# A fused state-space and expert layer: new instruction orders in its first six and last three groups, and more identity products on TensorE at the start

## The reference, cut to what matters

```python
mod = (_silu(L0_c) @ L0_wmod).reshape(8, 6, 1, -1)
sa, ca, ga, sb, cb, gb = ...                     # ga, gb: kept at least 0.25 from zero
h = _layernorm(x) * (1 + ca) + sa
# state part
v, gate = split(h @ W_in + b_in)
hs[t] = sigmoid(A) * hs[t-1] + v[t]              # a scan over the 1024 rows of a batch
x = x + ga * ((sigmoid(gate) * hs * C) @ W_out + b_out)
# expert part
h = _layernorm(x) * (1 + cb) + sb
p = softmax(h @ gate_w + gate_b); p = p * (p >= 0.1); p = p / sum(p)
x = x + gb * sum_e p[:, e] * (h @ expert_w[e] + expert_b[e])     # 8 experts
```

## Time and profile before

| what | value |
|---|---|
| median of 3 runs | 209.23 us (208.98 to 212.89) |
| the profiled execution, its own time | 209.71 us |
| its span, first to last instruction | 207.9 us |
| busy: PE, DVE, ACT, POOL | 192.8, 188.9, 180.5, 169.0 us |

### The profile page before, as it was taken

How to read it: one execution, slowest core, us unless ns; L and a number is a source line. 1 busy time by engine, 2 the same in 40 slices (tenths; PEclk the granted TensorE clock), 3 DMA queues, 4 the chain that set the end, 5 groups by cost and what they waited for, 6 DMA issues and landing times.

```text
span 207.9 us, 4221 instructions
## 1 busy us (share of the span) xinstructions
PE 192.8 (93%) x951; PEld 142.7 (69%) x951; DVE 188.9 (91%) x840; ACT 180.5 (87%) x596; POOL 169.0 (81%) x216
## 2 busy tenths in 40 slices
PE   6998979999999999999999999999999999989930
PEld 6764358676776868686867787777778686667710
DVE  2878996999998999999999999999999999698994
ACT  3527259999999999999999999999999999999940
POOL 8158999677999898979898988898988948877860
PEclk9999999999999999999999999999999999999985
DMA  6710121301111111112111101111010101001103
GB/s 194 211 33 2 50 60 26 110 15 53 38 50 50 57 50 50 50 50 55 52 52 43 53 16 55 39 52 54 2 50 0 54 2 52 2 0 54 39 13 101
DMA packets 20114, 10.34 MB, mean 50 GB/s; under 512 B 1369, under 2 KB 19938, under 8 KB 20090
## 3 DMA queue, kind: packets, MB, share of 16 engines
q1 hardware_dynamic: 20072, 10.07, 17.0%
q10 hardware_dynamic: 18, 0.00, 0.0%
HBM read 5.81 MB, written 4.26 MB: 48 GB/s over the span
## 4 chain that ended last, share of the span: by engine, by line
PE 72%; ACT 12%; DVE 10%; issue 2%; DMA 2%; DVEq 0%; SPq 0%; ACTq 0%
PE ring L1790 11%; PE ring L1791 11%; PE ring L1792 11%; PE bank_a L1729 7%; PE bank_v L1714 7%; ACT z L718 6%; PE bank_g L1720 6%; PE bank_g L1766 3%; PE bank_a L1675 3%; PE bank_g L1765 3%; ACT xn L731 3%; PE bank_g L1675 2%; PE bank_v L1710 2%; DMA wmod<-in_L_wmod_dram 2%; PE bank_v L1807 1%
## 5 line engine op out<-in xcount | busy, mean ns | idle before, releaser
L718 ACT ACTIVATE z<-ring,wts 128x128 f32<-128x128 f32 x436 | 122.3, 414 | 2.6 <-PE ring L1792 1.1
L517 POOL TENSOR_TENSOR z<-z 128x512 f32<-128x512 f32 x45 | 59.3, 1322 | 15.7 <-ACT z L718 15.7
L1790 PE MATMUL ring<-expert_w_hi,h_hi 128*128 128x512 f32 x128 | 59.2, 463 | 0.1
L1792 PE MATMUL ring<-expert_w_hi,h_lo 128*128 128x512 f32 x128 | 50.6, 395 | 0.0
L1791 PE MATMUL ring<-expert_w_lo,h_hi 128*128 128x512 f32 x128 | 50.4, 394 | 0.0
L525 POOL TENSOR_TENSOR z<-z 128x512 f32<-128x512 f32 x31 | 39.7, 1297 | 5.5 <-DVE z L1053 5.2
L496 POOL TENSOR_SCALAR xn<-x_in,neg_mean,rstd 128x128 f32<-128x128 f32 x60 | 26.6, 458 | 6.9 <-DVE rstd L992 6.6
L1790 PEld LDWEIGHTS ring<-expert_w_hi,h_hi 128*128 128x128 f32 x128 | 24.2, 189 | 8.5 <-issue 4.2
L1791 PEld LDWEIGHTS ring<-expert_w_lo,h_hi 128*128 128x128 f32 x128 | 24.2, 189 | 6.7 <-issue 3.3
L1792 PEld LDWEIGHTS ring<-expert_w_hi,h_lo 128*128 128x128 f32 x128 | 24.1, 188 | 5.7
L731 ACT ACTIVATE xn<-x,shift,rstd 128x128 f32<-128x128 f32 x60 | 25.6, 558 | 0.0
(11 more groups left out here) (122 smaller groups left out, 384.6 us busy)
## 6 DMA issues: line engine op xcount, KB each, us to landing
x_in<-in_L_attn_x_dram SPq DMA_DIRECT2D x16, 256.0 KB, 2.8
out_dram<-x SPq DMA_DIRECT2D x15, 256.0 KB, 2.3
expert_w<-in_L_ffn_expert_w_dram SPq DMA_DIRECT2D x2, 256.0 KB, 3.9
wmod<-in_L_wmod_dram SPq DMA_DIRECT2D x1, 384.0 KB, 4.6
expert_b_parts<-b_hi SPq DMA_DIRECT2D x8, 32.0 KB
out_dram<-x SPq DMA_DIRECT2D x2, 128.0 KB, 1.9
w_in<-in_L_attn_W_in_dram SPq DMA_DIRECT2D x1, 128.0 KB, 4.9
expert_b_parts<-b_lo SPq DMA_DIRECT2D x4, 32.0 KB
```

The costliest lines, as they stand in the source:

```text
L517: nc.gpsimd.tensor_tensor(z[:, g % 2, t, 0:4, :], z[:, g % 2, t, 0:4, :], z[:, g % 2, t, 4:8, :], ALU.add).then_inc(folded[t], 1)
L718: last = nc.scalar.activation(z[:, g % 2, t, e, :], bank_k[:, (e % 4) * P:(e % 4 + 1) * P], ACT.Copy, scale=wts[:, g % 2, t, e:e + 1])
L1790: mm(bank_k[:, :], hi, expert_w_hi[:, cols], start=True, stop=False)
L1792: mm(bank_k[:, :], lo, expert_w_hi[:, cols], start=False, stop=True).then_inc(e_ready[k], 1)
```

## The change

No instruction of the computation is added or taken away. Four things differ:

1. `keep_clock`: 39 products in place of 11. The groups are 5 (start), 5 (behind `turn_silu`), 3 (behind `turn_xn1(0)`), 1 (ahead of `gate_rows`), and three that have no counterpart in the kernel before: 9 ahead of `turn_xn2(0)`, 14 between `turn_xn2(0)` and `turn_xn1(2)`, 2 ahead of `logits(0)`. These three write to banks that others use, so the 14 stand behind the wait for x1 of group 1, and the 2 behind the wait for the fourth `gates_out`.
2. The order of the prologue: `silu` comes before the first statistics on DVE; `first_norm(0)` comes ahead of the statistics of group 1 and of `modulation(0)`; `turn_xn1(0)` comes ahead of `modulation_columns(1)` on PE; `gate_input(0)` ahead of `state_input(0)`; on ACT `pick_rows(1)` comes ahead of `skip_columns`, and `expert_high` ahead of `gates_out(0)`.
3. The fill is written out for six groups in place of four, with new places for halves, weighings, folds and router steps. On PE and ACT the loops begin at s = 6 in place of 4, with the same order inside.
4. Groups 12 to 15 have a new order of halves and of what reads them. The last half on PE is (15, 3) in place of (15, 0).

The core of the diff on PE:

```diff
-            keep_clock(ring[0], 6)
+            keep_clock(ring[0], 5)
             turn_silu()
-            keep_clock(ring[0], 1)
+            keep_clock(ring[0], 5)
             modulation_columns(0)
             modulation_rows()
+            turn_xn1(0)
+            keep_clock(ring[0], 3)
             modulation_columns(1)
-            keep_clock(ring[0], 2)
-            turn_xn1(0)
-            keep_clock(ring[0], 2)
+            gate_input(0)
             state_input(0)
-            gate_input(0)
+            keep_clock(ring[0], 1)
             gate_rows()
...
             after_gate(1)
+            keep_clock(bank_g, 9)
             turn_xn2(0)
             after_product(1)
+            keep_clock(bank_a, 14)
             turn_xn1(2)
+            after_gates()
+            keep_clock(ring[3], 2)
             logits(0)
```

and of ACT and DVE:

```diff
+            bias_rows_copy(1)
             exponentials(0)
-            gates_out(3)
+            second_norm(1)
             gate(2)
-            second_norm(1)
+            weigh(0, 0)
             weigh(0, 5)
-            weigh(0, 0)
...
-HALF_STEPS = (4, 12)
+HALF_STEPS = (6, 12)
...
             half(15, 1)
-            half(15, 3)
+            half(15, 0)
             after_parts(14)
             turn_parts(15)
-            half(15, 0)
+            half(15, 3)
```

More of the change, by code:

```diff
@@ L580, in _ @@
             add_pairs(2, 0)
-            for s in range(3, 11):
+            for s in range(3, 12):
                 fold(s, 1)
@@ L803, in _ @@
             h2_high(4)
-            for s in range(4, 12):
+            weigh(3, 2)
+            weigh(3, 3)
+            h1(6)
+            weigh(3, 5)
+            weigh(3, 4)
+            exponentials(4)
+            gate(6)
+            weigh(3, 0)
+            weigh(3, 1)
+            second_norm(5)
+            weigh(4, 6)
+            parts_out(3)
+            h2_high(5)
+            weigh(4, 3)
+            weigh(4, 2)
+            h1(7)
+            weigh(4, 5)
+            weigh(4, 4)
+            exponentials(5)
+            weigh(4, 0)
+            gate(7)
+            weigh(4, 1)
+            second_norm(6)
+            weigh(5, 6)
+            parts_out(4)
+            h2_high(6)
+            for s in range(6, 12):
                 weigh(s - 1, 2)
@@ L1405, in _ @@
             root(5, 0)
-            for s in range(4, 11):
+            add_bias(2)
+            root(5, 1)
+            logit_sum(4)
+            root(5, 2)
+            times_gb(2)
+            router(4, 0)
+            result(2)
+            router(4, 1)
+            root(5, 3)
+            root(5, 4)
+            root(5, 5)
+            root(5, 6)
+            router(4, 2)
+            router(4, 3)
+            x_stats(8, 1)
+            router(4, 4)
+            root(5, 7)
+            negated_mean(5)
@@ new lines, in _ @@
+            root(5, 8)
+            router(4, 5)
+            shifts(5)
+            scan(6)
+            router(4, 6)
+            gated(6)
+            x_stats(8, 2)
+            router(4, 7)
+            weigh_onto(3, 7, 0)
+            weigh_onto(3, 7, 1)
+            weigh_onto(3, 7, 2)
+            x_stats(8, 3)
+            weigh_onto(3, 7, 3)
+            first_residual(6)
+            x1_stats(6)
+            low_part(5)
+            moments(6)
+            sum_pairs(3, 1)
+            sum_pairs(3, 0)
@@ new lines, in _ @@
+            root(6, 0)
+            add_bias(3)
+            logit_sum(5)
+            root(6, 1)
+            router(5, 0)
+            root(6, 2)
+            times_gb(3)
+            router(5, 1)
+            root(6, 3)
+            result(3)
+            x_stats(9, 0)
+            root(6, 4)
+            root(6, 5)
+            root(6, 6)
+            negated_mean(6)
+            router(5, 2)
+            root(6, 7)
+            router(5, 3)
+            root(6, 8)
+            router(5, 4)
@@ new lines, in _ @@
+            x_stats(9, 1)
+            router(5, 5)
+            shifts(6)
+            scan(7)
+            router(5, 6)
+            gated(7)
+            weigh_onto(4, 7, 0)
+            router(5, 7)
+            weigh_onto(4, 7, 1)
+            weigh_onto(4, 7, 2)
+            x_stats(9, 2)
+            x_stats(10, 0)
+            weigh_onto(4, 7, 3)
+            first_residual(7)
+            x_stats(9, 3)
+            x1_stats(7)
+            low_part(6)
+            moments(7)
+            sum_pairs(4, 1)
@@ L1407, in _ @@
+            sum_pairs(4, 0)
+            root(7, 0)
+            for s in range(6, 11):
                 add_bias(s - 2)
@@ L1904, in _ @@
             gate_input(5)
+            half(2, 1)
             after_bias(1)
```

544 lines of the change are left out of this document (290 added, 254 removed), and 10 rows, old and new, of tables (FIRST_HALVES, LAST_HALVES).

## The result

| | before | changed |
|---|---|---|
| median of the runs taken together | 209.3 us (208.98 to 212.89, 4 runs) | 212.85 us (211.48 to 213.55, 4 runs) |
| profiled execution, its span | 209.71, 207.9 us | 213.55, 211.6 us |

The ratio is 1.0174, 95% interval 1.0144 to 1.0203: 3.6 us slower. The forecast of 210.2 us was 2.65 us too low, and its range ended at 212.7 us.

The account below looks back on a forecast made before the run. PE and ACT were taken as full from 70 to 170 us, ACT then DVE after, so the first half sets the end. 209.7 + 2.5 - 1.2 - 0.3 = 210.7 us, given as 210.2 against the median; range 207.0 to 212.7 us.

Parts of the forecast that it names:

- The clock rose early: Prologue on PE: clock up by 10.4 us instead of about 13.6, L1812 at about half of 1.93 us.
- first output product: End of the prologue on PE: near 16.8 us in place of 17.99, a term of -1.2 us.
- The first half: First expert half on PE, behind the 25 later products: 2.5 us later, near 33.4 us.
- Their worth here is zero: The 25 later products ahead of the first half: no cold matmuls to save, the clock holds through the 1.06 us gap.
- The fill, -1.2 us: Fill up to 70 us: PE gives up waits for ACT, leaving PE and ACT both about 1.3 us late.
- ACT's first weighing: Fill on ACT: 1.35 us later than before, thus less late than PE at 2.5 us.
- The first rival: Products cost little because POOL or DVE is later and PE would stand anyway: 206.7 us, or 208 partly paid; chance 0.22.
- The tail, -0.3 us: From 170 to 190 us: a better order gives at most ACT's 0.32 us of idle time; behind 190 us, 0.
- a bad order: Tail behind 190 us on DVE: could cost about 0.7 us, one half.
- +2.5: Term for the 25 later products (5.5 us) on PE: the first half 2.5 us later.
- the second: Rival: new orders recover nothing, the whole delay reaches the end, 211.7 us, up to 213; chance 0.20.
- the two signs that the prediction had set: Loop at 70 us: 1.3 us behind if the forecast holds, 2.5 us behind if the second rival does.

Follow-up runs that it names:

- e7: Changed kernel without its 25 later products, with the tail of before and expert_bias_low ahead of first_norm(3) on POOL: 208.84 us.
- e9: As e7, with three identity products just ahead of the first logits: 207.17 us.
- e11: Changed kernel with all 39 products, with expert_bias_low ahead of first_norm(3) on POOL and the tail of before: 210.89 us.
- e13: As e9, with POOL's biased_input(4) moved behind fold(1, 1): 206.13 us.
- e2: Kernel before with 25 identity products added, 9 ahead of turn_xn2(0) and 16 ahead of turn_xn1(2): 213.27 us.
- e6: Kernel before with the new orders of groups 12 to 15 alone: 210.12 us.
- e12: Kernel before with three identity products ahead of the first logits, the last gates_out moved ahead of h1(2) on ACT: 209.5 us.

## Why the prediction was wrong

**Right.** The clock rose early (L1812 1.02 us where 1.93 stood), the first output product came 1.65 us earlier (forecast 1.2, the extra 0.45 makes the first half 2.0 us late and not 2.5). The nine products took 2.01 us and the fourteen 3.13 us from start to start, 0.22 each, without idle time, and the logits came at 29.62 us (forecast 30.1). The first half was awaited near 33.4 us and came at 32.26; the forecast had named the end of the gate product there, in before 30.84 us, while the half starts at 30.29. From 70 to 170 us nothing moved.

**"Their worth here is zero."** Wrong in kind, though it cost the sum nothing: without any, the clock falls in most executions (1.3 us at the first half, 1.7 us between the medians of e7 and e9). But 25 of them cost 3.7 us (e11 against e9), and three in the idle stretch do the work.

**The fill, -1.2 us.** This is the step that failed. The forecast let the first half be 2.5 us late and the loop 1.3; measured were 1.97 and 3.15 us, so the term was +1.2 us. One part of its reasoning came true: ACT's first weighing was 1.13 us later (forecast 1.35), less than PE's 1.97. What PE got back is 0.8 us (e11), and e9 has the same 0.8 us with no delay to make up, so it belongs to the new order; with the sums free it is 1.7 us (e13). What turned it round is that I had not walked POOL's and SP's queues past the moved `expert_bias_low`: `first_norm(3)` ahead of it waits 3.88 us, 12 issues and group 6's load stand behind it. In the profiled execution this turned -0.8 into +1.2 us: 1.2 us of wait for the load, and about 0.7 us because the sums then fell beside two instructions of POOL and not one. The first rival named POOL's order, but as a help to the products.

**The tail, -0.3 us.** It was +0.55. I had bounded it by ACT's idle time and priced a bad order by one half; what became late was DVE, by sums that tripled beside POOL. Behind it ACT's 0.32 us of idle time became 1.18. With the sums moved the same order gained 0.4 us, a little more than forecast.

**The sum.** Against the profiled execution of before, the forecast had +2.5 - 1.2 - 0.3 = +1.0 us, and measured were +2.0 + 1.2 + 0.55, the 3.7 us of the span.

**The rivals.** By number it was the second, "the whole delay reaches the end" with 211.7 to 213 us. By mechanism it was so in e2. The changed kernel lands there by chance: 2.0 us of first half, -0.8 of fill, +2.0 of late load with the sums it pushed beside POOL, and +0.55 of tail. Its loop ran 3.15 us behind, more than either of the two signs that the prediction had set (1.3 and 2.5).

## What to carry to other kernels

Before products that keep the clock are put in, find the stretch in which the engine is idle, and fill that and no more: what stands over delays a queue in order. Of every step that moves, walk the queue behind it on each engine, SP's issues too. And look where a VectorE instruction with two SBUF inputs falls beside one of GpSimd: an order that looks equal on paper was worth 1 us twice here.

## What the runs showed of the hardware that was not expected

A 128x256 sum of two SBUF tensors on DVE takes 0.41 us alone and 0.95 to 1.51 us when it begins well inside a 128x512 sum of POOL that reads SBUF, while the 128x512 sums with one operand in a PSUM bank took 0.67 to 0.70 us throughout. A stretched sum shows as busy and not as waiting. The early rise of the clock varies: with the new prologue the first gate product took 1.1 us at 9.7 to 11.1 us in every profile, but with the order of before the first state product took 1.93, 1.93, 1.63 and 1.43 us at 11.3 to 12.2 us (before, e2, e6, e12), and in e2 L1720 still took 1.87 us at 12.99 us. In e2 the clock had been up and fell again; windows with the granted clock in the seventh column:

```profile
5.00:8.00 3.00, 2.19 (x18) 1.78 (x16) 2.79 (x25) 1.93 (x6) 0.91 (x3) 0.97 0.65 164
8.00:11.00 3.00, 2.15 (x11) 1.89 (x9) 2.86 (x16) 1.51 (x2) 0.00 (x0) 0.50 0.94 265
```

PE went through the products of the modulation there, from 5.03 us on, with a wait of 0.81 us in their midst. Why the clock falls ahead of the first half only in profiles with the new prologue (three of three without late products, neither of the two with the prologue of before) stays open.
